# Moving the key-list turns and the round-end work inside the gather of a five-round graph network kernel

## The reference

```python
def _L0_gnn_ref(x, edge_index, edge_attr, weight, w_ih, w_hh, b_ih, b_hh):
    src, dst = edge_index[0], edge_index[1]
    h = x
    for i in range(5):
        m = h @ weight[i]
        msgs = m[src] * edge_attr[:, None]
        agg = segment_sum(msgs, dst, num_segments=n_nodes)
        h = gru_cell(agg, h, w_ih, w_hh, b_ih, b_hh)
    return h
# gru_cell: gi = agg @ w_ih.T + b_ih; gh = h @ w_hh.T + b_hh
# r, z = sigmoid(i_r + h_r), sigmoid(i_z + h_z); n = tanh(i_n + r * h_n)
# h' = (1 - z) * n + z * h
x = x + _L0_gnn_ref(_layernorm(x), edge_index, edge_weight, ...)
x = x + ffn(...); x = x + graph_attention(_layernorm(x), src, dst, ...); x = x + ffn(...)
```

## Time and profile before

| what | value |
|---|---|
| device time, three runs | 5827.36, 5843.19, 5851.38 us |
| span of the profiled execution | 6333.9 us |
| TensorE busy (matmuls) | 4494.3 us, 71% |
| VectorE busy | 2762.3 us, 44% |
| GpSimd busy | 2376.8 us, 38% |
| ScalarE busy | 1765.6 us, 28% |

### The profile page before, as it was taken

How to read it: one execution, slowest core, us unless ns; L and a number is a source line. 1 busy time by engine, 2 the same in 40 slices (tenths; PEclk the granted TensorE clock), 3 DMA queues, 4 the chain that set the end, 5 groups by cost and what they waited for, 6 DMA issues and landing times. The chain is left out here.

```text
span 6333.9 us, 62448 instructions
## 1 busy us (share of the span) xinstructions
PE 4494.3 (71%) x17139; PEld 2678.1 (42%) x17139; DVE 2762.3 (44%) x6296; ACT 1765.6 (28%) x4059; POOL 2376.8 (38%) x2811
## 2 busy tenths in 40 slices
PE   1111314258999999999998985477777776997798
PEld 0011101024544544544544464355555554664464
DVE  7994000024264344353214024444444446777435
ACT  4332000000000000000001313344554545997121
POOL 3787777720000000000001013666666664886023
PEclk9999555579899999999999988788888887998697
DMA  8700211137432222221333243666666663776323
GB/s 356 290 1 26 83 66 59 58 125 257 138 111 97 89 91 77 104 92 61 114 108 100 82 128 95 179 200 196 195 197 194 198 196 116 243 242 212 122 64 108
DMA packets 381651, 866.06 MB, mean 137 GB/s; under 512 B 87403, under 2 KB 187654, under 8 KB 353931
## 3 DMA queue, kind: packets, MB, share of 16 engines
q1 hardware_dynamic: 250843, 687.06, 31.1%
q0 software_dynamic: 76816, 147.75, 9.1%
q10 hardware_dynamic: 53664, 27.26, 1.5%
HBM read 577.75 MB, written 284.11 MB: 136 GB/s over the span
## 5 line engine op out<-in xcount | busy, mean ns | idle before, releaser
L1110 PE MATMUL PS<-mem 128*128 128x512 f32 (+1 forms) x3500 | 1460.5, 574 | 396.1 <-issue 354.3
L1110 PEld LDWEIGHTS PS<-mem 128*128 128x128 f32 x3500 | 655.8, 201 | 1176.1 <-issue 1130.7
L2027 POOL DMA_INDIRECT mem<-gat_rows,mem x832 | 814.0, 978 | 527.0 <-issue 451.4
L1291 POOL TENSOR_TENSOR mem<-mem 128x256 f32<-128x256 f32 x25 | 20.2, 841 | 2136.7 <-DMA mem<-x 2136.7
L581 POOL DMA_INDIRECT adjacency_more<-mem x526 | 541.9, 1030 | 172.2 <-issue 172.2
L2070 PE MATMUL PS<-mem 128*128 128x256 bf16 x2496 | 434.7, 305 | 176.0 <-issue 165.4
L1176 ACT ACTIVATE mem<-PS 128x512 f32<-128x512 f32 (+1 forms) x35 | 19.0, 544 | 1916.9 <-PE PS L1110 1357.8
L2135 DVE TENSOR_TENSOR mem<-mem,PS 128x512 f32<-128x512 f32 x416 | 285.4, 686 | 608.2 <-ACT mem L2108 485.8
L2438 PE MATMUL PS<-mem 128*128 128x264 f32 x1660 | 461.8, 407 | 7.6 <-DVE mem L2389 3.2
L2103 ACT ACTIVATE PS<-PS 128x512 f32<-128x512 f32 x416 | 245.1, 589 | 700.0 <-remote 513.0
L262 PE MATMUL PS<-mem 106*128 106x106 f32 (+4 forms) x446 | 102.0, 374 | 476.5 <-DVE mem L393 302.4
(11 more groups left out here) (407 smaller groups left out, 7068.1 us busy)
## 6 DMA issues: line engine op xcount, KB each, us to landing
mem<-adjacency SPq DMA_DIRECT2D x150, 1280.0 KB
gathered_rows<-mem SPq DMA_DIRECT2D x416, 264.0 KB
mem<-gathered_rows SPq DMA_DIRECT2D x208, 528.0 KB, 4.5
adjacency<-mem SPq DMA_DIRECT2D x56, 800.0 KB, 20.7
adjacency_more<-mem SPq DMA_DIRECT2D x56, 800.0 KB
mem<-adjacency_more SPq DMA_DIRECT2D x30, 1280.0 KB
adjacency<-mem SPq DMA_DIRECT2D x30, 1280.0 KB
mem<-edge_slots ACTq DMA_DIRECT2D x26, 1024.0 KB
```

The source lines that it names most:

```text
L1110: ins = t.matmul(PS[:, f, 0:n], lhsT=h[:, b, f * 128:(f + 1) * 128], rhs=m.pan[i % NPAN][:, j, 0:n], start=(b == 0), stop=(b == NB - 1))
L2027: g.indirect_dma_start(m.Dg[i % RING][:, k, j, :], None, HD[:, :], bass.IndirectOffsetOnAxis(ap=L.idxD[:, c:c + 1], axis=0)).then_inc(s[f" ...
```

## The change

Three things change. (1) The two halves of a list turn go to two banks, 7 and 2, and both are issued behind one wait. (2) The toN turn of a level moves from ahead of the gather to behind the gather's first fifth, with a wait that the gates before have been read from bank 2; the gates behind that gather wait until VectorE has read both halves of the level's last turn (`turned_until`). (3) The turns of a round's last two blocks, b = 23 and 24, move behind the first and the second fifth of the next round's first gather, and that round's weight products (now in `rounds_products`) behind its third fifth. Round 0's products stay ahead of its first gather.

```diff
--- before.py
+++ after.py
@@ -688,6 +688,7 @@
 
 
 BANK = 7
+HALF_BANKS = (7, 2)
 LAST_LEVEL = 10
 KEYS, BLOCKS, WITHIN, LEVELS_AT = 0, 1, 2, 2
 
@@ -740,11 +741,11 @@
     if back:
         i, n = i + level + 1, n + level
     t.wait_ge(*s["keys"](n))
+    t.wait_ge(*s["turned"](1 + 2 * turn))
     parts = list(turn_parts(m, "toT" if back else "toN", m.K[i % 2], 0))
     for h in range(2):
-        t.wait_ge(*s["turned"](1 + 2 * turn + h))
         for src, (_, rows, cols) in parts[4 * h:4 * h + 4]:
-            ins = into(t, PS, (src, (BANK, rows, cols)), ident)
+            ins = into(t, PS, (src, (HALF_BANKS[h], rows, cols)), ident)
         ins.then_inc(s["kt"].sem, 1)
 
 
@@ -837,7 +838,7 @@
     for where, steps in (("toN", level), ("toT", 7)):
         for h in range(2):
             v.wait_ge(*s["kt"](2 * turn + h + 1))
-            turn_half(v, m, cn, PS, where, level, m.K[(i + 1) % 2], BANK, h).then_inc(s["turned"].sem, 1)
+            turn_half(v, m, cn, PS, where, level, m.K[(i + 1) % 2], HALF_BANKS[h], h).then_inc(s["turned"].sem, 1)
         i, turn = i + 1, turn + 1
         for e in range(steps, 0, -1):
             kind = "flip" if where == "toN" and e == level else "plain"
@@ -882,7 +883,7 @@
     v.wait_ge(st.sem, st.n)
     v.wait_ge(*s["seg"](1))
     for h in range(2):
-        _, _, dst, src = half_turned(m, "toN", m.ki, PS, BANK, h)
+        _, _, dst, src = half_turned(m, "toN", m.ki, PS, HALF_BANKS[h], h)
         v.wait_ge(*s["kt"](2 * NTURN + h + 1))
         v.tensor_copy(dst, src).then_inc(s["turned"].sem, 1)
     v.wait_ge(*s["turned"](2 * NTURN + 3))
@@ -1056,23 +1057,10 @@
 def rounds_tensor(t, m, cn, s, PS, lm, li):
     ident = cn.ident
     t.wait_ge(*s["ht"](NB))
+    rounds_products(t, m, s, PS, 0)
     for l in range(5):
-        t.wait_ge(*s["wt"](16 * (l + 1)))
-        t.wait_ge(*s["w"](96))
-        for f in range(2):
-
-            if l:
-                t.wait_ge(*s["rz_read"](NB * l))
-                t.wait_ge(*s["nn_read"](NB * l))
-            for lo, hi, bank in ((0, 512, 2 + f), (512, 768, 4 + f)):
-                for k in range(2):
-                    ins = t.matmul(PS[:, bank, 0:hi - lo], lhsT=m.wt[:, k, f * 128:(f + 1) * 128],
-                                   rhs=m.wih[:, k, lo:hi], start=(k == 0), stop=(k == 1))
-                ins.then_inc(s["wi_ps"].sem, 1)
         for q in range(NG + 1):
             level = level_at(l, q - 1) if q else None
-            if level:
-                lists_turn(t, lm, li, PS, ident, 2 * level - 2)
             if q < NG:
                 rounds_gather(t, m, s, PS, l, q, ident, lm, li, level)
                 if q and listed_at(l, q - 1) == KEYS:
@@ -1081,12 +1069,32 @@
                 p = q - 1
                 t.wait_ge(*s["agg_v"](NG * l + p + 1))
                 t.wait_ge(*s["agg_a"](NG * l + p + 1))
+                if level:
+                    t.wait_ge(*li["turned"](turned_until(level)))
                 for b in range(4 * p, min(4 * p + 4, NB)):
                     rounds_gates(t, m, s, PS, l, b)
-                    if b and l < 4:
+                    if b and l < 4 and b < NB - 1:
                         rounds_turn(t, m, s, PS, l, b - 1, ident)
-        if l < 4:
-            rounds_turn(t, m, s, PS, l, NB - 1, ident)
+
+
+def turned_until(level):
+
+    return 1 + 4 * min(level, LAST_LEVEL) + (2 if level > LAST_LEVEL else 0)
+
+
+def rounds_products(t, m, s, PS, l):
+
+    t.wait_ge(*s["wt"](16 * (l + 1)))
+    t.wait_ge(*s["w"](96))
+    if l:
+        t.wait_ge(*s["rz_read"](NB * l))
+        t.wait_ge(*s["nn_read"](NB * l))
+    for f in range(2):
+        for lo, hi, bank in ((0, 512, 2 + f), (512, 768, 4 + f)):
+            for k in range(2):
+                ins = t.matmul(PS[:, bank, 0:hi - lo], lhsT=m.wt[:, k, f * 128:(f + 1) * 128],
+                               rhs=m.wih[:, k, lo:hi], start=(k == 0), stop=(k == 1))
+            ins.then_inc(s["wi_ps"].sem, 1)
 
 
 def rounds_gather(t, m, s, PS, l, q, ident, lm, li, level):
@@ -1110,8 +1118,15 @@
                 ins = t.matmul(PS[:, f, 0:n], lhsT=h[:, b, f * 128:(f + 1) * 128], rhs=m.pan[i % NPAN][:, j, 0:n],
                                start=(b == 0), stop=(b == NB - 1))
         ins.then_inc(s["panel_used"].sem, 1)
+        if k == 0 and level:
+            t.wait_ge(*s["rz_read"](NB * l + 4 * (q - 1)))
+            lists_turn(t, lm, li, PS, ident, 2 * level - 2)
         if k == 2 and level and level <= LAST_LEVEL:
             lists_turn(t, lm, li, PS, ident, 2 * level - 1)
+        if l and q == 0 and k < 2:
+            rounds_turn(t, m, s, PS, l - 1, NB - 2 + k, ident)
+        if l and q == 0 and k == 2:
+            rounds_products(t, m, s, PS, l)
 
 
 def rounds_gates(t, m, s, PS, l, b):
```

## The result

The changed kernel takes 5744.7 us (median; 5732.0 to 5773.8) against 5847.1 us of the kernel before on the same runs: 0.983 of its time, 95% interval 0.981 to 0.986, so 97 us less with an interval of 81 to 113 (the two medians, of five executions each, lie 102 us apart). The prediction was 5750 us, 93 us less.

A forecast was written before the change was run, and what follows sets the result against it. TensorE's queue was taken to bound rounds 1 to 4. Terms 55 + 1.6 + 14.5 + 21.8 = 93 us, carried over as microseconds: 5843 - 93 = 5750 us, range 5727 to 5785.

The forecast's parts named there:

- What bounds: Rounds 1 to 4: they end when TensorE ends, busy in 1669 of 1736 us; shortening its queue shortens the kernel.
- The layers behind shift with it: Layers behind the rounds: they begin when the last states are there, so everything behind keeps its old length.
- List turns, levels 1, 2, 4 to 7, 9, 10: List turns behind gates: both waits and the loss behind go, 6.3 us in four levels, 7.4 in four, 55 us.
- Levels 3 and 8: List turns behind a gather without gates: waits go, the next gather waits 1.0 us; net 0.8 us each, 1.6 together.
- Level 11: Its list turn: the 11.81 us wait for ten key instructions and the loss behind it go, 14.5 us.
- Round ends: Last row turns and weight products of four rounds: the 3.3 us wait and loss behind it go, 21.8 us together.
- The losses of 1.27 and 2.36 us: Records behind the 3.96 us waits of list turns: time lost against an undisturbed 25.96 us, four levels of either kind.
- The low clock stays: Rival at the moved turns: each leaves the low clock behind it, only waits return, 65 us, 5778 us; chance 0.06.
- A new wait for the compares: Rival at high levels' toT turns, if comparing exceeds 3.6 us slack at level 10: 69 us gain, 5774 us; chance 0.05.
- Slower: the clock falls under unbroken load: Rival in rounds 1 to 4: without pauses the granted clock falls, at 0.84 the time is 6057 us; chance 0.03.
- The gain is given back: Rival: panel loads set the round ends, or the next layer starts no earlier; 5843 us, at most 15 off; chance 0.05.
- the 491 us: Profiled execution's excess over the plain runs' median: most or all put in round 0, whose matmuls stand 2.8 us apart.

The follow-up runs named there:

- part (3) alone: Changed kernel with the list turns of before, so only the round ends moved; 0.996 of the kernel before, stretch of rounds 1 to 4 1733.6 us.
- turns_ahead: Changed kernel with toN turns ahead of the gather except in levels 3 and 8, weight products behind the fifth fifth; 0.984 of the kernel before, stretch 1650.4 us.
- filled_waits: Kernel before, with unused matmuls put into TensorE's wait between the halves of toN turns (four in eight levels, thirteen in level 11); stretch 1733.9 us, 19.9 less.
- filled_steps: Kernel before, with unused matmuls in the toN waits differing by level: three, two, one or none, thirteen in level 11; stretch 1740.6 us.

## Why the prediction was right

**What bounds.** TensorE's queue set the end of rounds 1 to 4, and what left it came off the kernel's time in full: 98 us of the stretch, 97 us (81 to 113) of the device time. "The layers behind shift with it" held: 2634 us behind the stretch with and without the change.

**List turns, levels 1, 2, 4 to 7, 9, 10.** 6.3 or 7.4 us each were worked out, 55 in all; measured were 59. Levels 1 and 2 gained 51.39 - 44.57 = 6.8 us and, from 52.48, 7.9 us. The mechanism was right, the term was 0.5 us short each: I kept the transposes at the time that they take when a wait cuts them in two, 0.52 + 0.42 us for toN and 0.59 + 0.52 us for toT, and as eight in a row they take 0.72 and 0.87 us. This is most of the 5 us by which the sum was too small.

**Levels 3 and 8.** Net 0.8 us was worked out, with a new wait of 1 us between the gathers. The four waits of 0.99 us are there, and 1.25 us each were gained (a round's first gates come 1.25 us earlier than in part (3) alone). `turns_ahead` shows that this wait was all that the new order left on the table, but for one wait of 0.9 us in round 1.

**Level 11.** 14.5 us were worked out. The step went from 58.46 us (2861.14 to 2919.60) to 43.69 (2565.18 to 2608.87 in the changed kernel's timeline), 14.8 us. VectorE's ten key instructions now run beside the gather.

**Round ends.** 21.8 us were worked out, and the part alone gave 20.2 in the stretch. At the ends themselves it gave 22.2; the 2.0 us between are in the list turns, which stay in that kernel and whose clock losses came out longer there.

**What the clock costs.** The losses of 1.27 and 2.36 us behind a wait were taken from rows and called the lower clock, without proof. `filled_waits` is the proof: 19.9 us come back with every read as late as before, and the granted clock behind the turns is 1.00. The split into four levels of either kind was no property of the levels, however: in part (3) alone and in `filled_steps` the same levels lose other amounts. The sum over the list turns held to 2.0 us, a single level not to one.

**The rivals.** *The low clock stays* falls: transposes stand inside the gathers in 11 toN turns, 10 toT turns and 8 row turns, and the clock is 1.00 over 1656 us. The Trainium skill, "TensorE: Matmul & The Clock Gate", part 4 (PE-mode transpose), says that the full clock doesn't engage for transposes; the traces show that up to 0.9 us of transposes among matmuls doesn't take it away, and no run here has a long stretch of transposes alone. The Trainium skill, "TensorE: Matmul & The Clock Gate", section "HAM oscillation — how this bites in real kernels", says that pauses for data bring the clock down and the work behind starts slow; the trace agrees for the waits of 3.96 us, 27.23 us behind them against 25.96 with `filled_waits`. *A new wait for the compares* falls for the third fifth, and its point of decision was right within 0.4 us. VectorE is idle for 4.24 us ahead of level 10's toT turn, where about 4 was said:

```profile
2508.24 1.67 DVE L734 TENSOR_TENSOR mem<-PS,mem 128x416 f32<-128x416 f32 x2 [5.53 <-PE PS L262]
...
2526.24 1.29 DVE L734 TENSOR_TENSOR mem<-PS,mem 104x512 f32<-104x512 f32 x2 [4.24 <-PE PS L262]
```

*Slower: the clock falls under unbroken load* falls with the 1.00 at 1651 busy microseconds of 1656. *The gain is given back* falls with the third stretch.

**One step was wrong.** I put most or all of the 491 us between the first profile and the plain runs in round 0. About half of it lay there (219 us up to round 0's end, against the changed kernel's profile) and half in the layers behind (244 us). The forecast didn't suffer, because it carried over microseconds of the stretch and not a ratio of the span. Scaled by 5843 / 6334, the 93 us would have been 86.

**What the prediction didn't see** is that its second part, the move of the toN turn, was idle. It costed the change as a whole and said that both waits go by two banks together with "a fifth of the gather" ahead of them. The first did it alone. Whether either would wasn't asked. The numbers for it were in the trace: VectorE's last read of the gates' banks ended at 1952.02, the turn came at 1953.07.

## What to carry to other kernels

Two halves of a job through one bank cost the producer the consumer's whole backlog, not only the read, when the first read is queued behind other work; a second bank took away all of it at both places tried, and moving the job alone only shortened it. Price a wait of some microseconds on TensorE with what it costs behind it, here 1.3 to 2.4 us on 4.0. Where a wait can't be removed, look for work to put into it: useful work gave 4.9 us here, and even matmuls for nothing gave 19.9 us of clock back, where a second bank gave 79. When an expensive stage sits between two noisy ones, measure that stage in the trace: its length repeats within 0.5 us in two profiles of the kernel before, where the device time of one kernel spreads by 20 to 40.

## What the runs showed of the hardware

The same kernel before took 5871 us (5865 to 5884, 12 runs) in one group of runs and 6318 us (6305 to 6346, 9 runs) in another, which ran on another chip, and rounds 1 to 4 don't know of it: the stretch of the two profiles of the kernel before is 1753.3 and 1753.8 us, with 494 us between their spans. The other kernels fit the same sums in both groups (1733.9 us for `filled_waits` in the second, with 1733 worked out). In the profiles of the second group, round 0 shows TensorE's matmuls 2.8 us apart with nothing waited for, while GpSimd issues its scatters. The first profile of the kernel before, 6333.9 us long, has the same picture; from its timeline of all engines:

```profile
716.89 0.96 POOL L581 DMA_INDIRECT adjacency_more<-mem  x1 [0.30 <-issue]
716.98 1.01 PE L1110 MATMUL PS<-mem 128*128 128x512 f32 x1 [2.21 <-issue]
...
719.78 1.01 PE L1110 MATMUL PS<-mem 128*128 128x512 f32 x1 [1.79 <-issue]
```

From its second profile, taken in the first group, TensorE's timeline at the same place:

```profile
708.32 8.86 PE L1110 MATMUL PS<-mem 128*128 128x512 f32 x20 [0.16 <-DVE mem L1245]
720.12 5.40 PE L1110 MATMUL PS<-mem 128*128 128x512 f32 x8 [2.94 <-DVE mem L1245]
```

There, 20 records take 8.86 us, and the idle time ahead of the rows is a wait for VectorE's L1245. (The last row is cut off at 725 us.) The waits of round 0's gather, from 680 us to the round's end, in the first and in the second profile:

```profile
PE PS L1110 <- issue: 354.3, 115, 90.7
PE PS L1110 <- DVE mem L1245: 424.1, 22, 134.4
```

The second profile has none for "issue". Why the matmuls stand apart in the second group was not tried, and with one chip for each group nothing tells the chip from the time of the runs. Ratios are alike in both (0.983 and 0.984 for kernels 5 us apart in the stretch).

That two idle times of 3.09 us on TensorE, one list level apart, cost 1.5 us and nothing, was the other thing not expected.
